# A transformer block with cross attention and eight experts: the start of the program laid anew

## What is computed

```python
def block(x, ctx, mask, W_q, b_q, W_k, b_k, W_v, b_v, W_o, b_o, Wp, sim, temp, W1, b1, W2, b2):
    q = heads(layernorm(x) @ W_q.T + b_q)                    # 16 heads of 8
    k, v = heads(ctx @ W_k.T + b_k), heads(ctx @ W_v.T + b_v)
    s = where(mask == 0, -inf, q @ k.T / sqrt(8))            # 128 x 77 a head
    x = x + merge(softmax(s) @ v) @ W_o.T + b_o
    n = layernorm(x)
    g = l2norm(n @ Wp.T) @ l2norm(sim).T / temp              # 8 scores a token
    comb = softmax of the two largest of g, 0 elsewhere
    h = gelu(n @ W1[e] + b1[e])                              # 128 -> 512, e = 0..7
    return x + sum over e of comb[e] * (h @ W2[e] + b2[e])
```

## Time and profile before

| | us |
|---|---|
| median of 3 runs | 399.42 |
| lowest and highest | 399.18 and 400.06 |
| the profiled execution, its own time | 399.57 |
| its span, first to last instruction | 397.8 |

### The profile page before, as it was taken

How to read it: one execution, slowest core, us unless ns; L and a number is a source line. 1 busy time by engine, 2 the same in 40 slices (tenths; PEclk the granted TensorE clock), 3 DMA queues, 4 the chain that set the end, 5 groups by cost and what they waited for, 6 DMA issues and landing times.

```text
span 397.8 us, 14194 instructions
## 1 busy us (share of the span) xinstructions
PE 346.5 (87%) x3564; PEld 294.1 (74%) x3565; DVE 304.0 (76%) x972; ACT 291.6 (73%) x845; POOL 277.9 (70%) x495
## 2 busy tenths in 40 slices
PE   3639999999999999999998669999999999999800
PEld 2317777787777877777776559999999999999800
DVE  5056899999999999999999755677666566668873
ACT  3238999999999999999998646566666666666521
POOL 5431347777777777777765475789999888789872
PEclk9958999999999999999999968999999999999965
DMA  5920001111011110130000031222322222249246
GB/s 140 399 66 24 24 2 44 44 44 45 26 43 42 42 40 22 48 96 20 21 29 16 31 89 29 70 69 70 81 79 73 82 67 70 64 118 279 71 127 190
DMA packets 39049, 29.18 MB, mean 73 GB/s; under 512 B 5107, under 2 KB 34751, under 8 KB 39008
## 3 DMA queue, kind: packets, MB, share of 16 engines
q1 hardware_dynamic: 31120, 18.60, 16.3%
q0 software_dynamic: 4384, 8.60, 6.7%
q10 hardware_dynamic: 3504, 1.51, 1.4%
HBM read 17.53 MB, written 11.62 MB: 73 GB/s over the span
## 4 chain that ended last, share of the span: by engine, by line
PE 55%; DVE 21%; issue 9%; ACT 2%; DVEq 2%; DMA 2%; POOL 2%; POOLq 0%; SPq 0%; ACTq 0%
PE ps_s L894 16%; PE ps_s L905 14%; PE ps_t L641 6%; PE ps_o L652 3%; DVE sums L1198 3%; PE ps_s L625 3%; DVE mx L1181 3%; PE ps_s L615 3%; DVE rows L1266 2%; PE ps_t L887 2%; PE ps_x L672 1%; DMA ys<-results 1%; PE ps_o L666 1%; DVE x L1220 1%; DVE st L1230 1%
## 5 line engine op out<-in xcount | busy, mean ns | idle before, releaser
L561 POOL DMA_INDIRECT results<-eo,didx x71 | 70.8, 996 | 21.4 <-POOL didx L550 9.6
L894 PE MATMUL ps_s<-xtT,w1c 128*128 128x128 f32 x568 | 78.2, 282 | 1.0 <-DVE xtT L1594 0.9
L448 POOL DMA_INDIRECT lists<-rows,slots x64 | 66.6, 1041 | 17.6 <-issue 16.7
L905 PE MATMUL ps_s<-w2s,hT 128*128 x568 | 75.6, 277 | 0.2 <-ACT hT L1122 0.2
L950 ACT ACTIVATE pT<-ps_t 77x512 f32<-77x512 f32 x128 | 73.8, 593 | 2.5 <-PE ps_t L641 2.5
L641 PE MATMUL ps_t<-identf,pr 128*77 128x128 f32 x512 | 74.4, 280 | 0.4 <-ACT pT L950 0.3
L894 PEld LDWEIGHTS ps_s<-xtT,w1c 128*128 128x128 f32 x568 | 71.5, 198 | 2.0 <-DVE xtT L1594 2.0
L1118 ACT ACTIVATE w1c<-w1s 128x512 f32 x71 | 44.8, 631 | 34.8 <-PE ps_s L894 33.3
L905 PEld LDWEIGHTS ps_s<-w2s,hT 128*128 128x128 f32 x568 | 69.5, 193 | 0.5 <-issue 0.4
L1608 DVE TENSOR_TENSOR h<-ps_s,b1T 128x512 f32<-128x512 f32 x71 | 49.0, 690 | 25.0 <-PE ps_s L894 23.1
L641 PEld LDWEIGHTS ps_t<-identf,pr 128*77 128x77 f32 x512 | 60.4, 151 | 6.4 <-issue 4.7
(11 more groups left out here) (206 smaller groups left out, 620.0 us busy)
## 6 DMA issues: line engine op xcount, KB each, us to landing
xt<-lists SPq DMA_DIRECT2D x71, 66.0 KB
ys<-results SPq DMA_DIRECT2D x14, 256.0 KB, 4.1
xin<-in_x_dram SPq DMA_DIRECT2D x16, 128.0 KB
w1s<-in_L_ffn_W_dram SPq DMA_DIRECT2D x1, 2048.0 KB, 10.3
out_dram<-x SPq DMA_DIRECT2D x5, 256.0 KB, 5.8
cin<-in_ctx_dram SPq DMA_DIRECT2D x16, 77.0 KB
results<-eo,didx POOLq DMA_INDIRECT x71
lists<-rows,slots POOLq DMA_INDIRECT x64, 2.4
```

Of the source, the lines that this page charges most:

```text
L448: nc.gpsimd.indirect_dma_start(lists, bass.IndirectOffsetOnAxis(ap=slots[:, r, s * TOPK + k:s * TOPK + k + 1], axis=0), rows[:, r, s, k, : ...
L561: nc.gpsimd.indirect_dma_start(results, bass.IndirectOffsetOnAxis(ap=didx[:, r:r + 1], axis=0), eo[:, r, :], None, bounds_check=TOPK * NTO ...
L894: last = nc.tensor.matmul(ps_s[:, r, c * P:(c + 1) * P], w1c[:, r, c * P:(c + 1) * P], xtT[:, r, :], start=True, stop=True)
L905: last = nc.tensor.matmul(ps_s[:, 2 + r, 0:D], hT[:, r, c * P:(c + 1) * P], w2s[:, bass.ds(e + c * D, D)], start=(c == 0), stop=(c == FC - 1))
```

## The change

The loads of the prologue are shared out anew. ACT issues W_k, W_q, b_q, W_v, W_o; SP issues x and context of pair 0, b_k, the mask, x and context of pair 1, and then b_v, b_o, W_p, b1, the gate's matrix and the temperature; POOL issues none of them. The experts' weights go out one expert at a time, `w1` and `w2` of expert e ahead of the load of pair e + 5 in SP's program, `b2s` ahead of that of pair 13, with 17 increments of `l_ffn` instead of 3. DVE takes the first statistics of pair 0 ahead of the head mask and of the memset of `rows`, and in its step 0 the statistics of pair 2 stand behind the maxima and subtractions. PE's, ACT's and POOL's first steps are written out in a new order: W_q and W_k are turned apart from W_v and W_o, the masks of batch 0 come ahead of the turn of x, W_p and b1 are turned behind the queries, and context, values and keys of pair 1 come behind the first scores. The computation stays as it was.

```diff
@@ -55,6 +55,8 @@
     AHEAD = 3
+    AFTER = 3
+    FFN_LOADS = 2 * NE + 1
     DRAINED = 9
@@ -349,17 +351,26 @@
             step(0, 0)
-            sp.dma_start(wnat[:, 1, :], w_k).then_inc(l_w, 16)
-            sp.dma_start(wnat[:, 0, :], w_q).then_inc(l_w, 16)
-            sp.dma_start(simn[:, :], sim).then_inc(l_sim, 16)
-            sp.dma_start(b1n[:, :], b1.rearrange("e (c f) -> (e c) f", f=P)).then_inc(l_sim, 16)
+            sp.dma_start(bk[:, :], b_k.rearrange("(p o) -> p o", o=1)).then_inc(l_bk, 16)
             sp.dma_start(maski[:, :], mask.rearrange("a b q k -> (a b q) k")).then_inc(l_mask, 16)
             step(1, 1)
-            sp.dma_start(w1s[:, :].rearrange("p (e f) -> p e f", e=NE), w1.rearrange("e d f -> d e f")).then_inc(l_ffn, 16)
-            sp.dma_start(w2s[:, :].rearrange("p (e c d) -> p e c d", e=NE, c=FC),
-                          w2.rearrange("e (c p) d -> p e c d", p=P)).then_inc(l_ffn, 16)
-            sp.dma_start(b2s[:, :], b2.rearrange("e d -> (e d)").partition_broadcast(P)).then_inc(l_ffn, 16)
-            steps(sp, step, RING, NP - 1, RING, NP - 1)
+            sp.dma_start(bv[:, :], b_v.rearrange("(p o) -> p o", o=1)).then_inc(l_bvo, 16)
+            sp.dma_start(bo_row[:, :], b_o.partition_broadcast(P)).then_inc(l_bvo, 16)
+            sp.dma_start(wnat[:, 4, :], w_p).then_inc(l_later, 16)
+            sp.dma_start(b1n[:, :], b1.rearrange("e (c f) -> (e c) f", f=P)).then_inc(l_later, 16)
+            sp.dma_start(simn[:, :], sim).then_inc(l_later, 16)
+            sp.dma_start(tempc[:, :], temp.partition_broadcast(P)).then_inc(l_later, 16)
+
+            def expert_weights(i):
+                e = i - RING - AFTER
+                if 0 <= e < NE:
+                    sp.dma_start(w1s[:, e * F:(e + 1) * F], w1[e, :, :]).then_inc(l_ffn, 16)
+                    sp.dma_start(w2s[:, e * F:(e + 1) * F].rearrange("p (c d) -> p c d", c=FC),
+                                 w2[e, :, :].rearrange("(c p) d -> p c d", p=P)).then_inc(l_ffn, 16)
+                elif e == NE:
+                    sp.dma_start(b2s[:, :], b2.rearrange("e d -> (e d)").partition_broadcast(P)).then_inc(l_ffn, 16)
+
+            steps(sp, step, RING, NP - 1, RING + AFTER + NE, NP - 1, RING, expert_weights)
@@ -432,13 +443,6 @@
-
-            pool.dma_start(bo_row[:, :], b_o.partition_broadcast(P)).then_inc(l_rows, 16)
-            pool.dma_start(tempc[:, :], temp.partition_broadcast(P)).then_inc(l_rows, 16)
-
-            pool.wait_ge(zeroed, N_ZEROS)
-            pool.wait_ge(headmask4_ready, 1)
-
             def scatter(J, m, s, k):
@@ -539,8 +538,15 @@
-            step(-2, -2)
-            step(-1, -1)
+            first_power(0, 0)
+            pool.wait_ge(headmask4_ready, 1)
+            keys_by_head(0, 0)
+            first_power(1, 1)
+            pool.wait_ge(bo_ready, 1)
+            residual_start(0, 0)
+            residual_start(1, 1)
+            similarity()
+            pool.wait_ge(zeroed, N_ZEROS)
             steps(pool, step, 0, 17, 5, 13)
@@ -590,18 +596,6 @@
         def _(pe):
-
-            pe.wait_ge(l_w, 16 * 5)
-            pe.wait_ge(consts, N_CONSTS)
-            for n in range(4):
-                last = nc.tensor.transpose(ps_t[:, 0, n * P:(n + 1) * P], wnat[:, n, :], identf[:, :])
-            last.then_inc(wt_done, 1)
-            nc.tensor.transpose(ps_t[:, 1, 0:P], wnat[:, 4, :], identf[:, :])
-            pe.wait_ge(l_sim, 16 * 2)
-            nc.tensor.transpose(ps_t[:, 1, P:P + NE * FC], b1n[:, :], identf[0:NE * FC, 0:NE * FC]).then_inc(wt_done, 1)
-            pe.wait_ge(wt_copied, 1)
-            pe.wait_ge(l_bqk, 16 * 3)
-            nc.tensor.matmul(ps_t[:, 0, 0:D], bv[:, 0:1].to_broadcast([P, P]), woT, start=True, stop=True).then_inc(bvo_done, 1)
@@ -869,14 +861,40 @@
-            step(-1, -1)
-            step(0, 0)
+            pe.wait_ge(consts, N_CONSTS)
+            pe.wait_ge(l_wqk, 16 * 2)
+            nc.tensor.transpose(ps_t[:, 0, 0:P], wnat[:, 0, :], identf[:, :])
+            nc.tensor.transpose(ps_t[:, 0, P:2 * P], wnat[:, 1, :], identf[:, :]).then_inc(wt_done, 1)
+            turn_context(0, 0)
+            pe.wait_ge(wt_copied, 1)
+            pe.wait_ge(l_wvo, 16 * 3)
+            nc.tensor.transpose(ps_t[:, 0, 2 * P:3 * P], wnat[:, 2, :], identf[:, :])
+            nc.tensor.transpose(ps_t[:, 0, 3 * P:4 * P], wnat[:, 3, :], identf[:, :]).then_inc(wt_done, 1)
+            keys(0, 0)
+            pe.wait_ge(mask_ready, 1)
+            masks(0, 0)
+            pe.wait_ge(wt_copied, 2)
+            pe.wait_ge(l_bvo, 16 * 2)
+            nc.tensor.matmul(ps_t[:, 0, 0:D], bv[:, 0:1].to_broadcast([P, P]), woT, start=True, stop=True).then_inc(bvo_done, 1)
+            after(pe, E["k_ready"], 0)
+            turn_x(0)
+            queries(0)
+            pe.wait_ge(l_later, 16 * 4)
+            nc.tensor.transpose(ps_t[:, 1, 0:P], wnat[:, 4, :], identf[:, :])
+            nc.tensor.transpose(ps_t[:, 1, P:P + NE * FC], b1n[:, :], identf[0:NE * FC, 0:NE * FC]).then_inc(wt_done, 1)
+            scores(0, 0, 0)
+            turn_context(1, 1)
+            after(pe, E["cT_ready"], 1)
+            values(0, 0)
+            after(pe, E["v_ready"], 0)
+            keys(1, 1)
+            masks(0, 1)
             pe.wait_ge(bo_ready, 1)
             pe.wait_ge(tab_ready, 3)
-            pe.wait_ge(l_ffn, 16 * 3)
+            pe.wait_ge(l_ffn, 16 * FFN_LOADS)
             ps_u = [ps_t[:, 0, :], ps_t[:, 1, :]]
@@ -930,18 +948,13 @@
         def _(act):
-            for n, w in ((2, w_v), (3, w_o), (4, w_p)):
-                act.dma_start(wnat[:, n, :], w).then_inc(l_w, 16)
-            act.dma_start(bk[:, :], b_k.rearrange("(p o) -> p o", o=1)).then_inc(l_bqk, 16)
-            act.dma_start(bq[:, :], b_q.rearrange("(p o) -> p o", o=1)).then_inc(l_bqk, 16)
-            act.dma_start(bv[:, :], b_v.rearrange("(p o) -> p o", o=1)).then_inc(l_bqk, 16)
-            act.wait_ge(consts, N_CONSTS)
+            for n, w in ((1, w_k), (0, w_q)):
+                act.dma_start(wnat[:, n, :], w).then_inc(l_wqk, 16)
+            act.dma_start(bq[:, :], b_q.rearrange("(p o) -> p o", o=1)).then_inc(l_wvo, 16)
+            for n, w in ((2, w_v), (3, w_o)):
+                act.dma_start(wnat[:, n, :], w).then_inc(l_wvo, 16)
+            act.wait_ge(consts, 6)
             nc.scalar.activation(warm[:, :], neghalf[:, :], ACT.Exp)
-            act.wait_ge(wt_done, 1)
-            nc.scalar.activation(wT[:, :, :].rearrange("p n m -> p (n m)"), ps_t[:, 0, :], ACT.Copy).then_inc(wt_copied, 1)
-            act.wait_ge(l_bqk, 16 * 3)
-            act.wait_ge(l_sim, 16 * 2)
-            nc.scalar.activation(sim_sq[:, :], simn[:, :], ACT.Square, accum_out=sim_n2[:, 0:1]).then_inc(sim_sqd, 1)
@@ -1094,17 +1107,30 @@
-            act.wait_ge(zeroed, N_ZEROS)
+            act.wait_ge(wt_done, 1)
+            nc.scalar.activation(wT[:, 0:2, :].rearrange("p n m -> p (n m)"), ps_t[:, 0, 0:2 * P], ACT.Copy).then_inc(wt_copied, 1)
+            context_out(0, 0)
+            act.wait_ge(wt_done, 2)
+            nc.scalar.activation(wT[:, 2:4, :].rearrange("p n m -> p (n m)"), ps_t[:, 0, 2 * P:4 * P], ACT.Copy).then_inc(wt_copied, 1)
+            act.wait_ge(l_bk, 16)
+            keys_out(0)
+            first_norm(0, 0)
+            x_out(0)
             act.wait_ge(bqs_ready, 1)
-            step(-1, -1)
-            act.wait_ge(wt_done, 2)
+            queries_out(0, 0)
+            act.wait_ge(l_later, 16 * 4)
+            nc.scalar.activation(sim_sq[:, :], simn[:, :], ACT.Square, accum_out=sim_n2[:, 0:1]).then_inc(sim_sqd, 1)
+            act.wait_ge(wt_done, 3)
             nc.scalar.activation(wg[:, 0:D], ps_t[:, 1, 0:P], ACT.Copy).then_inc(wpt_copied, 1)
             nc.scalar.activation(b1T[:, 0:NE * FC], ps_t[:, 1, P:P + NE * FC], ACT.Copy).then_inc(wpt_copied, 1)
-            steps(act, step, 0, 17, 5, 14)
+            context_out(1, 1)
+            first_norm(1, 1)
+            act.wait_ge(zeroed, 1)
+            steps(act, step, 1, 17, 5, 14)
             nc.scalar.activation(expd[:, 0:PART], diff[:, 0:PART], ACT.Exp).then_inc(exp_ready, 1)
-            act.wait_ge(l_ffn, 16 * 3)
+            act.wait_ge(l_ffn, 16 * FFN_LOADS)
             act.wait_ge(tab_ready, 3)
@@ -1160,13 +1186,6 @@
             nc.vector.memset(ones16[:, :], 1.0).then_inc(zeroed, 1)
-            nc.vector.memset(rows[:, :, :, :, :], 0.0).then_inc(zeroed, 1)
-            dve.wait_ge(zeroed, N_ZEROS)
-            dve.wait_ge(consts, N_CONSTS)
-            nc.vector.tensor_reduce(headmask4[:, :], headmask[:, :].rearrange("p (g j) -> p j g", g=G), AX.X, ALU.add
-                                    ).then_inc(headmask4_ready, 1)
-            dve.wait_ge(l_bqk, 16 * 3)
-            nc.vector.tensor_scalar(bqs[:, :], bq[:, :], SCALE, None, ALU.mult).then_inc(bqs_ready, 1)
@@ -1446,7 +1465,7 @@
                     tables(0, 7)
-                if has(J, 2):
+                if has(J, 2) and not (known(J) and J == 0):
```

(16 more changed lines are left out.)

11 lines of the change are left out of this document (2 added, 9 removed).

## The result

The changed kernel has a median of 389.44 us in 4 runs (386.44 to 390.84). The kernel before, run beside it, has 399.74 (399.18 to 400.45). The ratio is 0.9731, with a 95% interval of 0.9672 to 0.9791. The profiled execution is the fastest of the four: its own time is 386.44 us.

What follows compares the result with a forecast made beforehand. The prediction took a late start to bound the kernel: a hole near 20 us, carried through a full steady state. 399.57 - 8.25 (1.2 of it from the first part) = 391.3, median 391.2 us; range 388.6 to 393.3.

Steps and rivals of the forecast that it cites:

- The hole: Near 20 us: pair 2's statistics idle DVE 12.15 us for a load behind the weights; its end moves 8.25 us earlier.
- The steps to the second scores: Start-up walk through loads, PE, ACT and DVE: second scores start at 18.4 instead of 26.65.
- the sum: Whole kernel: 8.25 us off gives 391.2 us, clock rise moved along to 25.5 us; 62 in 100, range 390.0 to 392.3.
- This part gives 1.2 us: First loads to first scores: reordered prologue starts scores at 12.7 instead of 13.93; bounds 0 and 2 us.
- Two of the signs that I named for this stretch: Before the second scores: masks released by ACT's exponentials near 18, and no DVE wait over 2 us.
- whatever the start gives or takes is carried to the end one for one: Full steady state: nothing there catches up a late start, so the 8.25 us shift reaches the end.
- the clock rises early: Rival, before the second scores: denser PE work raises the clock, 1.5 to 2.5 us more off, 388.8 to 389.8; 16 in 100.
- by the row it does not: Start-up: durations read as 1.2 GHz until 33.7 us, so no early rise, which would take some 2 us more off.
- Another load in the hole's place: Rival, start-up: pair 3's x or bo's inputs arrive late, giving back 1 to 3 us, 392.3 to 394.3; 13 in 100.
- a cover of 0.8 us: DVE step 1: pair 3's statistics end at 19.0, DVE needed at 19.8; a 4.1 us load would cost 0.7.
- Spread weights: SP's queue from pair 4 on: 17 weight loads hidden in SP's wait, cost nothing; uncovered, up to 1.9 us per expert.
- The rival of 406 us: Pairs 5 to 12: spread weights delay x loads, 1.9 us in each of 8 steps, 7 us slower; 3 in 100.

Runs made afterwards that it cites:

- e2: The kernel before with only the experts' weights spread behind the pairs; 391.32 us, ratio 0.9776.
- e3: The kernel before with only pair 2's statistics moved behind step 0's maxima and subtractions, weights in bulk; 394.99 us, ratio 0.9890.
- e4: The changed kernel with the experts' weights in three bulk loads at their old place; 395.10 us, ratio 0.9899.
- e1: The changed kernel run once more with no edit; 390.60 us, ratio 0.9755 against the kernel before.
- e7: The changed kernel with 24 unread matmuls at PE's start and 24 more in PE's waits; 386.13 us, ratio 0.9663.
- e6: The changed kernel with 24 unread matmuls at PE's start; 390.39 us, ratio 0.9768.
- e8: The changed kernel with each expert's w1 and w2 loaded twice, SP waiting for the previous expert's loads; 391.18 us, ratio 0.9780.
- e12: e7 with 34 more unread matmuls at the turn to the experts; 398.27 us on a slower chip, ratio 0.9700.
- e9: The kernel before with 74 unread matmuls at the start and in PE's waits, PE also waiting for bo; 412.78 us on a slower chip, ratio 1.0047.
- e11: e7 with batch 0's masks behind the queries and 12 unread matmuls ahead of x's turn; 400.33 us on a slower chip, ratio 0.9712.
- e10: e9 with the experts' weights spread behind the pairs; 406.14 us on a slower chip, ratio 0.9884.

## Why the prediction was right, point by point

**The hole.** Right. The wait of DVE L1247 was for a load behind the weights, and it takes nothing but the weights' going to remove it (e2). With the weights in front, neither the moved statistics (e3) nor the whole new prologue (e4) removes it: both then end on the load at 22.2 to 22.4 us.

**The steps to the second scores**, in an execution with the clock that the sum assumed (e1):

| | predicted | e1 | before |
|---|---|---|---|
| x turned | 9.1 | 8.95 | 10.36 |
| first scores | 12.7 | 12.02 | 13.93 |
| x of pair 2 issued | 11.3 | 11.78 | 18.34 |
| first maxima | 14.2 | 13.56 | 22.87 |
| masks of batch 1 | 17.2 | 16.55 | 25.51 |
| scores of batch 1 | 18.4 | 17.72 | 26.65 |
| x of pair 3 issued | 15.9 | 15.01 | 19.54 |
| clock risen to stay | 25.5 | 25.0 to 25.3 | 33.7 |

The mis-sized term is the first part, "This part gives 1.2 us": it gave 1.9 at the first scores (13.93 - 12.02). x was turned when predicted. What was too long was the stretch from there to the scores, 3.07 us instead of the 3.57 that I took over from before. From x's turn to the queries it was 1.47 us before, with pair 1's context turned between them (10.36 to 11.83), and is 1.14 now. And the masks that left that stretch had not been hidden behind the copy of q: they ended at 14.00, when the scores began, while in e1 the scores begin 0.15 us after qT's end (11.40 + 0.47). I had read these rows, and said that their removal gives nothing. The 0.7 us of error at the second scores come from here, with 0.15 from x: the shift there is 8.93 us and not 8.25. That x came out right is in part luck. W_o landed at 6.38 and not near 5.7, so that the masks ended at 8.57 and not at 8.3, and the turn of x started 0.06 us before the bias product's end, where I had added the two up. The chain behind the first maxima was right to 0.1 us. The maxima start 1.5 us after the scores do, the masks 3.0 us later, the scores 1.2 after those. Two of the signs that I named for this stretch did not come as said, both without effect: the last mask did not wait for ACT's exponentials, which end at 17.03 in e1, and DVE had a wait of over 2 us after all, the 3.99 for PE's first scores, which is nobody's loss.

**What is carried on.** The last load of x in the program is issued at 172.25 us before, at 163.12 in e1, 9.1 us earlier. The shift of the second scores went through the steady state. In the profiled execution after, a shift of 10.80 us at the second scores (26.65 - 15.85) has become 13.78 at that load (158.47): it ran at the high level there, and before ran at the low one from the hole to 33.7 us. And a part of the start did not show in the end. e2 has none of the new prologue, has its second scores 1.5 us later than e1, and issues that load at 162.98, no later than e1. By their rows e2's clock had risen by 21.7 us, e1's at 25.0. So "whatever the start gives or takes is carried to the end one for one" holds only at the same clock. The prologue's part is worth 0.7 us in the medians of e1 and e2, and their intervals overlap: that it gives anything is not shown.

**The clock.** The rival "the clock rises early" had 16 in 100 and 388.8 to 389.8 us. It came in the profiled execution, and by more than I gave it: at 10 us and not just before the second scores. In numbers it is the difference between 386.44 and 391.11 us. That the cause is the clock and not another part of these executions is shown by e7, which holds the high level on purpose: 386.13, 4.3 us less than e6 on the same chip and by ratio 3.7 less than e1, with a last issue of x at 158.03. The intervals of e7 and of e1 don't overlap. The two executions of the changed kernel differ ahead of that load alone: behind it they have 226.23 and 226.18 us. The median of 389.44 is 1.8 us below my sum, below the sum's own range of 390.0 to 392.3 as well, and e1's is 0.6 below the sum. Which clock the executions at 389.2 to 390.2 had is the open question of e1. The Trainium skill (TensorE: Matmul & The Clock Gate, Part 1) says that the number of slow matmuls at a kernel's start differs from run to run; one program with its queries in 0.72 and in 1.22 us, both at 10.1, agrees.

What the Trainium skill says of release by sustained activity I set aside for "by the row it does not", and there I misread a row. The keys' 0.53 us at 17.34 do not fit the long durations. The same keys earlier in that execution:

```profile
8.59 0.85 PE L705 MATMUL ps_x<-cT,wT 128*128 128x154 f32 x2 [0.56 <-ACT cT L1008]
```

In e2, whose PE does the same work up to there at times within 0.04 us, they take 0.88 at 17.35; in e7 and in the profile after, with all else short, 0.53. So before, the clock had risen between 16.4 us, where the values end with the long 1.14, and 17.34, behind the dense stretch as that rule has it, and was lost again in the hole (0.50 from 20 to 25 us). PE did not run at 1.2 GHz "from the start to about 33.7 us". The sum did not suffer, as that rise was over before the second scores; this is luck. Before and e2, or e1 and the profile after, show that a rise can come or not come after the same work. The 2 us that I gave to the early rise were too small, too, since it shortens every matmul from 10 us on and not those behind the second scores alone.

**Another load in the hole's place.** x of pair 3 was to have a cover of 0.8 us. In e1 its statistics wait 0.39 us and start at 17.33, and DVE's next maxima are still released by PE, at 19.20. It cost nothing. This rival had no weight here, nor in e7, with all durations short: there the wait is 0.17 us, and PE releases the next maxima too.

**Spread weights.** Predicted at no cost; e8 doubles them and adds nothing that its profile or the spread of the runs shows. The two issues of one expert took up to 1.65 us against my bound of 1.51, and two of the 17 loads over the 1 us of issue that I had named as a sign (1.06 and 1.23), on a queue that idles for the rest of the step. From the load of x of pair 5 to that of pair 12, the steps that carry the weights, it is 87.81 us before (46.97 to 134.78) and 87.64 in e1 (38.01 to 125.65), and none of these seven steps is longer by more than 0.03. The rival of 406 us is out.

**What stays open.** Whether the turn to the experts can be filled with more profit than e12's 1.5 us at most. Why the part behind the last load of x takes 11 to 12 us longer on the third chip: e9 to e11 have it as well as e12, so it isn't e12's added matmuls. Why five of e4's twelve executions took 5 us more than the others. And how the clock ran in the executions of the changed kernel at 389.2 to 390.2 us.

## What to carry to other kernels

A wait that stands in front of an in-order engine is removed at the transfer and not at the instruction: with the bulk weights still ahead on the queue, moving the waiting statistics only passed the wait to the next maxima (e3, e4) and gave about half of the gain, while loads that nobody needs for 200 us cost nothing that could be measured once they are spread over a queue that idles. When holes are gone, look at matmul durations in the first 20 us of more than one execution: two executions here differ by 4.7 us for the clock alone. PE's short waits there can then be filled with unread matmuls (e7, 4.3 us against e6), but only on a start without a long hole (e9), ahead of the wait and not behind it (e10), and where they cost less than it lasts (e11).

## What the runs showed that I had not expected

The granted clock can rise and fall again within microseconds of the start. In e6 it was up at the first masks (0.69 us at 6.73) and down by the second scores (1.41 us at 15.33), and the mean of 0.69 over 14 to 16 us puts the fall near 14.8. In e4 queries and scores took 0.70 and 0.80 us at 10.05 and 11.47, and the masks at 15.22 took 1.23. In e3 the masks at 18.09 took 0.77 us and the turn of x at 20.08 took 0.69, the long form. After the fall it took long to come back: in e6 the next masks of 0.70 us are at 22.39, and in e4 those at 28.59 still take 1.21.

The mean clock of an execution is a poor guide to its start: the two profiled executions of the changed kernel have 0.966 each and are 4.7 us apart. And b2s, with two 2 MB loads ahead of it, held SP's own instruction stream at its issue for 11.23 to 11.57 us in the kernel before, e3 and e9, and for 9.71 in e4. That hold is what kept pair 2's load back; with the weights spread the issue took 0.36 us and the load landed in 4.8.
